# A graph network layer: the one-hots of gathered rows move from VectorE to GpSimd, a turn later, with the flags of used slots copied beside the row numbers

## The chip, the cores and the metric

The program runs on one core of a Trainium2 chip. The metric is the device time of one execution in microseconds (us). A core has the engines TensorE (PE in the profile; PEld is its weight load), VectorE (DVE), ScalarE (ACT), GpSimd (POOL) and SyncE (SP), which each work through a queue of their own in order and meet through semaphores.

## The reference

25,000 edges with sorted source nodes (`src` here is the row that sums go to) and 50,000 nodes of width 256.

```python
h = concat([x[row], x[col]])                      # 25000 x 512
msgs = silu(h @ W1.T + b1) @ W2.T + b2
agg = segment_sum(msgs, row) / (cnt + 1e-8)       # per node
gi, gh = agg @ w_ih.T + b_ih, x @ w_hh.T + b_hh   # 3 x 256 each
r, z = sigmoid(i_r + h_r), sigmoid(i_z + h_z)
n = tanh(i_n + r * h_n)
x_new = (1 - z) * n + z * x
y = gamma * (x_new - mean) / sqrt(var + 1e-5) + beta
out = layernorm(x + y)
```

## The kernel before

The work has two stages. The **edge stage** (to about 955 us) turns each edge into a message that is already multiplied by W2 and w_ih, and stores it in DRAM as one row of `messages`. It also makes a table: for each block of 128 nodes up to 126 slots, with the row of an edge in `slot_row` and a flag in `slot_used` that says whether the slot holds an edge. The **node stage** handles the nodes in 196 pairs of blocks, one pair in a turn of the loop `node_turns`. For a pair and each of its two halves (`h`), GpSimd gathers 126 message rows by an indirect DMA into `mg`. A one-hot matrix `oh` then says for each gathered row which of the 128 nodes it belongs to: row `i` compares `iota1` with the local node number that the message carries in column `LOC`, and multiplies by the flag. TensorE multiplies `oh` by `mg` (`segment_sum`), which adds each edge to its node, and then adds the products of x with w_hh into the same banks of PSUM (`products0`, `products1`).

Each engine runs its own list of parts in a turn. A part comes with a lag: at turn t it handles pair t + lag, so that a part with lag 4 works four pairs ahead. Nothing but the semaphores holds the engines together. The parts that matter here, in the order of a turn:

- POOL: `add_beta` (lag -2, xb = x + beta; it waits for the second gate of pair t-1, `n_rz1`), `gather_rows` (lag 4; at every second turn `copy_rows` first copies four columns of row numbers into `rows_now`), `inv_std1` (-2, every second turn) and `inv_std2` (-5), which raise a variance to the power -0.5 (rs in the trace).
- DVE: `gated_h` and `n_input` (-1; rhn and npre), `var_eps2` (-5), `residual` (-4, uu), `one_hot` (3), `minus_mean` (nm), `subtract_n`, `z_diff`, `x_new` (diff, zd, xn), `scale_gamma` (tg), `stats1` (st), `shift` (-5, nmr; a product of two 128x2 tiles that waits for rs of `inv_std2`), `aggregate1` (ag), and `var_eps1` at every second turn (ve<-ag).
- ACT: `last_norm` (-6, yy<-uu,nmr; it waits for nmr), `tanh` (-1; it waits for npre), `gates0` (0), `mean_scale` (1), `squares` (-4), `gates1` (0, rz).
- PE: `products0` (0), `segment_sum` (1; it waits for the one-hots and for npre of pair t-1, since the banks are two sets), `products1` (0).

In what follows a turn with even t (in which GpSimd copies row numbers) is called even, and the other odd.

Of the kernel before, what the change touches and what calls it, by code (L numbers as in the profile page):

```python
# [7 lines left out]
P = 128  # L8
# [55 lines left out]
def gnn_layer(nc, x, xt, src, dst, w1t, b1, w2, b2, wiht, whht, bih, bhh, gamma, beta, consts, out):  # L64
# [4 lines left out]
    with ctx:  # L69
        def sb(name, shape, dt=f32, until=ctx):  # L70
            return until.enter_context(nc.sbuf_tensor(name, shape, dt))

        def sem(name):
            return ctx.enter_context(nc.semaphore(name))
# [25 lines left out]
        gammab, betab = sb("gammab", [P, D]), sb("betab", [P, 2 * D])  # L100
        rows_now = sb("rows_now", [P, 2 * QU], i32)
        halves = sb("halves", [P, 4])
        top, levf, levi = sb("top", [P, 1]), sb("levf", [1, 1]), sb("levi", [1, 1], i32)
        levels = sb("levels", [1, 1], i32)

# [58 lines left out]
        rb_mm, rb_cp, rb_step, rb_ready = sem("rb_mm"), sem("rb_cp"), sem("rb_step"), sem("rb_ready")  # L164
        cn_ready, cn_mm, cn_cp, cn_put = sem("cn_ready"), sem("cn_mm"), sem("cn_cp"), sem("cn_put")

        idx_now = sem("idx_now")
        got_src, got_dst, e_stored = sems("got_src", XE), sems("got_dst", XE), sems("e_stored", EU)
        e_xt, e_hi, e_lo = sem("e_xt"), sem("e_hi"), sem("e_lo")
        e_hid, e_sil, e_sh, e_sl = sems("e_hid", KC), sems("e_sil", KC), sems("e_sh", KC), sems("e_sl", KC)  # L170
# [18 lines left out]
        def need(eng, s, value):  # L189
            if not isinstance(value, int) or value > 0:  # L190
                eng.wait_ge(s, value)  # L191
# [37 lines left out]
        def duo(q, u):  # L229
            return q // 2 + 1 if isinstance(q, int) else (q - u) // 2 + u // 2 + 1  # L230

        def node_turns(eng, parts, first, last):
            def step(q, u):
                for part, lag in parts:
                    if not isinstance(q, int) or 0 <= q + lag < PAIRS:
                        part(q + lag, (u + lag) % QU)

            head = QU * (-(min(lag for _, lag in parts) // QU) + 1)
            tail = PAIRS - QU * -(-max(lag for _, lag in parts) // QU)
            for q in range(first, head):  # L240
                step(q, q % QU)
            with eng.Fori(head // QU, tail // QU) as g:
                for u in range(QU):
                    step(g * QU + u, u)
            for q in range(tail, PAIRS + last):
                step(q, q % QU)
# [104 lines left out]
        @block.gpsimd  # L351
        def _(pool):
            last_row = pool.to_reg(EDGES_PAD - 1)
            pool.wait_ge(ld_e, 32)

            def gather_edges(t0, turn_no, side):
                if not isinstance(turn_no, int) or turn_no >= 2:
                    for u in range(XE):
                        pool.wait_ge(got_dst[u], 16 * (turn_no - 1))
                nc.gpsimd.tensor_copy(src_now[:, side, :], srci[:, bass.ds(t0, XE)]).then_inc(idx_now, 1)  # L360
                nc.gpsimd.tensor_copy(dst_now[:, side, :], dsti[:, bass.ds(t0, XE)]).then_inc(idx_now, 1)
                pool.wait_ge(idx_now, 2 * turn_no + 2)
                for u in range(XE):
                    need_apart(pool, pool_passed, e_xt, t0 + (u - XE + 1))
                    gather(xsrc[:, u, :], src_now[:, side, u:u + 1], x, got_src[u])
                    gather(xdst[:, u, :], dst_now[:, side, u:u + 1], x, got_dst[u])

            E_TURNS = TILES // XE
            gather_edges(0, 0, 0)
            nc.gpsimd.memset(halves[:, :], -0.5).then_inc(node_const, 1)  # L370
            with pool.Fori(0, E_TURNS // 2) as g:
                for side in range(2):
                    gather_edges((g * 2 + (side + 1)) * XE, g * 2 + (side + 1), (side + 1) % 2)

            for u in range(EU):
                pool.wait_ge(e_stored[u], 16 * (TILES // EU))
            pool.wait_ge(tab_ready, 1)
            pool.wait_ge(mg_zero, 2 * QU)

            def node_stage(summed):  # L380
                def copy_rows(q, u):
                    need(pool, S["n_oh"], q - QU + 2)
                    nc.gpsimd.tensor_copy(rows_now[:, 2 * u:2 * u + 4], slot_row[:, bass.ds(2 * q, 4)])\  # L383
                        .then_inc(idx_now, 1)
                    pool.wait_ge(idx_now, 2 * E_TURNS + duo(q, u))

                def gather_rows(q, u):
                    if u % 2 == 0 and not summed:
                        copy_rows(q, u)
                    for h in range(2):  # L390
                        to = mg[:, u, h, :].bitcast(f32)
                        need_apart(pool, pool_passed, S[f"n_sg{h}"], q - QU + 1)
                        if summed:
                            nc.gpsimd.dma_start(to, sums[h][bass.ds(q * P, P), :])\
                                .then_inc(got_m[2 * u + h], 16)
                        else:
                            gather(to, rows_now[:, 2 * u + h:2 * u + h + 1], messages, got_m[2 * u + h], last_row)

                def add_beta(q, u):

                    pool.wait_ge(S["n_rz1"], min(q + 2, PAIRS) if isinstance(q, int) else q + 2)
                    need(pool, S["n_u"], q - QU + 1)
                    pool.wait_ge(got_x[u], 16 * (nth(q, u) + 1))
                    nc.gpsimd.tensor_tensor(out=xb[:, u, :], in0=xs[:, u, :], in1=betab[:, :], op=ALU.add)\  # L404
                        .then_inc(S["n_xb"], 1)

                def inv_std1(q, u):
                    if u % 2 == 1:
                        pool.wait_ge(S["n_v1"], duo(q, u))
                        need(pool, S["n_u"], q - QU + 1)  # L410
                        nc.gpsimd.tensor_tensor(
                            out=rs1[:, u - 1:u + 1, :].rearrange("p q h -> p (q h)"),
                            in0=ve1[:, u - 1:u + 1, :].rearrange("p q h -> p (q h)"),
                            in1=halves[:, :], op=ALU.pow).then_inc(S["n_r1"], 1)

                def inv_std2(q, u):
                    pool.wait_ge(S["n_v2"], q + 1)
                    need(pool, S["n_y"], q - QU + 1)
                    nc.gpsimd.tensor_tensor(out=rs2[:, u, :], in0=ve2[:, u, :], in1=halves[:, 0:2], op=ALU.pow)\
                        .then_inc(S["n_r2"], 1)  # L420

                node_turns(pool, ((add_beta, -2), (gather_rows, 4), (inv_std1, -2), (inv_std2, -5)), first=-4, last=5)

            pool.wait_ge(ld_w, 16 * W_LOADS)
            pool.wait_ge(lv_ready, 1)
            n_levels = pool.value_load(levels[0:1, 0:1], min_val=1, max_val=MAX_LEVELS)
            with pool.If(n_levels > 1):
                with pool.Fori(0, n_levels) as lv:
                    with pool.Fori(0, BLOCKS) as b:
                        n = lv * BLOCKS + b  # L430
                        pool.wait_ge(v_rows, lv + 1)
                        pool.wait_ge(v_sum, n + 1)
                        nc.gpsimd.tensor_copy(rows_now[:, 0:1], slot_row[:, bass.ds(b, 1)]).then_inc(v_idx, 1)
                        need_apart(pool, pool_passed, v_idx, n + 1)
                        gather(mg[:, 0, 0, :].bitcast(f32), rows_now[:, 0:1], messages, v_got, last_row)
                pool.wait_ge(v_done, 1)
                pool.wait_ge(tab_ready, 2)
                node_stage(True)
            with pool.Else():
                node_stage(False)  # L440
# [106 lines left out]
        def _(dve):  # L547
# [243 lines left out]
                nc.vector.memset(slot_used[:, :], 1.0).then_inc(tab_ready, 1)  # L791
                dve.wait_ge(tab_ready, 2)

            def one_hot(q, u):
                for h in range(2):
                    need(dve, S[f"n_sg{h}"], q - QU + 1)
                    dve.wait_ge(got_m[2 * u + h], 16 * (nth(q, u) + 1))
                    last = nc.vector.tensor_scalar(oh[0:SLOTS, u, h, :], iota1[0:SLOTS, :],  # L798
                                                   mg[0:SLOTS, u, h, LOC:LOC + 1].bitcast(f32),
                                                   slot_used[0:SLOTS, bass.ds(q * 2 + h, 1)], ALU.is_equal, ALU.mult)  # L800
                last.then_inc(S["n_oh"], 1)

            def gated_h(q, u):
                dve.wait_ge(S["n_rz0"], q + 1)
                dve.wait_ge(S["n_rz1"], q + 1)
# [74 lines left out]
            def var_eps1(q, u):  # L880
                if u % 2 == 1:
# [1 line left out]
                    nc.vector.tensor_scalar(ve1[:, u - 1:u + 1, :], ag1[:, u - 1:u + 1, :, 1], EPS_LN, None, ALU.add)\  # L883
                        .then_inc(S["n_v1"], 1)

            node_turns(dve, ((gated_h, -1), (n_input, -1), (var_eps2, -5), (residual, -4), (one_hot, 3), (minus_mean, -4),
                             (subtract_n, -1), (z_diff, -1), (x_new, -1), (scale_gamma, -3), (stats1, -1), (shift, -5),
                             (aggregate1, -1), (var_eps1, -1)), first=-3, last=5)

        @block.tensor  # L890
        def _(pe):
# [193 lines left out]
```

## Time and profile before

| | |
|---|---|
| time, median of 3 | 2478.14 us (2478.11 to 2478.32) |
| the profiled execution | 2478.47 us, of which the span of its instructions is 2476.8 us |
| PE busy | 2301.0 us (93%) |
| DVE busy | 2122.0 us (86%) |
| ACT busy | 1496.2 us (60%) |
| POOL busy | 1332.4 us (54%) |
| granted TensorE clock, mean | 0.987 |

The chain in the page (the work that ended last, followed backwards) gives DVE 42% and PE 37% of the span. Busy time counts an instruction from its start to its end, also where it stands still in between. The interval from one xb on POOL to the next is one turn of the node stage.

### The profile page before, as it was taken

The numbers are of one execution on the slowest core, as the hardware profiler recorded it, in microseconds if no ns is written. First come the engines' busy times: TensorE is split into PE (matmuls) and PEld (weight loads), VectorE is DVE, ScalarE is ACT, GpSimd is POOL, SyncE is SP. The second block draws the span as 40 slices with busy tenths as digits, with TensorE's granted clock in tenths as the row PEclk, the third lists the DMA queues.
The fourth block names the chain that finished last, engine by engine and source line by source line (L and its number), as shares of the span: only waits on it lengthen the run. The fifth ranks groups of instructions, "written<-read, shape, count | busy, mean of one in ns | idle before, by whom it ended". The sixth has DMA issues, their size and how long they took to land.

```text
span 2476.8 us, 46628 instructions
## 1 busy us (share of the span) xinstructions
PE 2301.0 (93%) x10234; PEld 1622.0 (65%) x10234; DVE 2122.0 (86%) x6136; ACT 1496.2 (60%) x2955; POOL 1332.4 (54%) x1475
## 2 busy tenths in 40 slices
PE   4999999999999995999999999999999999999995
PEld 2888888888888883655555555555555555555553
DVE  4777777777777764899999999999999999999998
ACT  2444444444444442577767777777677777777776
POOL 3444444444444421566666666666666666666663
PEclk9999999999999997999999999999999999999998
DMA  3566666666666655666666666666666666666662
GB/s 105 213 232 227 229 230 228 230 227 231 225 233 225 234 209 193 200 216 216 213 210 213 214 217 205 216 207 210 203 212 213 210 205 212 215 209 212 209 204 94
DMA packets 192600, 520.31 MB, mean 210 GB/s; under 512 B 51362, under 2 KB 53946, under 8 KB 192572
## 3 DMA queue, kind: packets, MB, share of 16 engines
q1 hardware_dynamic: 117308, 313.53, 36.2%
q0 software_dynamic: 75264, 206.47, 25.5%
q8 instruction: 9, 0.15, 0.0%
q14 instruction: 19, 0.16, 0.0%
HBM read 468.02 MB, written 206.73 MB: 272 GB/s over the span
## 4 chain that ended last, share of the span: by engine, by line
DVE 42%; PE 37%; issue 15%; DVEq 3%; DMA 1%; ACT 1%; SPq 0%; POOL 0%; POOLq 0%; ACTq 0%
PE banks L893 34%; DVE zd L824 6%; DVE xn L830 5%; DVE st L871 5%; DVE diff L819 5%; DVE rhn L807 5%; DVE tg L835 4%; DVE uu L846 4%; PE banks L905 4%; DVE oh L798 3%; DVE ag L877 2%; DVE ve L860 1%; DVEq L798 1%; DVEq L191 1%; DVE nm L855 1%
## 5 line engine op out<-in xcount | busy, mean ns | idle before, releaser
L893 PE MATMUL banks<-whh,xts 128*128 128x512 f32 (+1 forms) x3136 | 1089.9, 485 | 0.0
L893 PEld LDWEIGHTS banks<-whh,xts 128*128 128x128 f32 x3136 | 552.4, 190 | 312.5 <-issue 281.7
L346 POOL DMA_INDIRECT mg<-messages,rows_now x392 | 408.1, 1041 | 170.4 <-POOL rows_now L383 87.1
L404 POOL TENSOR_TENSOR xb<-xs,betab 128x512 f32<-128x512 f32 x196 | 249.0, 1270 | 372.5 <-ACT rz L501 372.5
L346 POOL DMA_INDIRECT xsrc<-in_x,src_now x196 | 187.3, 956 | 438.5 <-PE banks L905 433.0
L893 PE MATMUL banks<-mg,oh 128*128 128x512 f32 (+1 forms) x1568 | 322.1, 348 | 108.7 <-issue 57.2
L893 PEld LDWEIGHTS banks<-mg,oh 128*128 128x128 f32 x1568 | 253.2, 189 | 214.9 <-issue 158.7
L525 ACT ACTIVATE yy<-uu,nmr,rs 128x256 f32<-128x256 f32 x392 | 214.0, 593 | 293.0 <-DVE nmr L866 293.0
L513 ACT ACTIVATE banks<-banks,rcount 128x768 f32<-128x768 f32 x392 | 326.7, 871 | 38.0 <-PE banks L893 24.9
L471 ACT ACTIVATE msg<-banks 128x512 fp32r<-128x512 f32 (+1 forms) x392 | 192.8, 492 | 246.7 <-PE banks L893 218.3
L625 DVE TENSOR_TENSOR msg<-banks,msg 128x512 fp32r<-128x512 f32 (+1 forms) x392 | 199.9, 552 | 160.1 <-issue 137.7
L893 PE MATMUL banks<-wsh,silh 128*128 128x512 f32 (+1 forms) x784 | 265.1, 338 | 2.9 <-DVE msg L625 2.9
L893 PE MATMUL banks<-bias_hn,ones 128*128 128x256 f32 x392 | 267.5, 682 | 0.0
L893 PE MATMUL banks<-wsh,sill 128*128 128x512 f32 (+1 forms) x784 | 263.8, 336 | 0.0
L893 PE MATMUL banks<-wsl,silh 128*128 128x512 f32 (+1 forms) x784 | 263.4, 336 | 0.0
L501 ACT ACTIVATE rz<-banks 128x512 f32<-128x512 f32 x392 | 229.3, 585 | 3.0 <-PE banks L893 3.0
L452 ACT ACTIVATE eh<-banks 128x512 fp32r<-128x512 f32 x196 | 117.5, 599 | 172.2 <-PE banks L905 172.2
L346 POOL DMA_INDIRECT xdst<-in_x,dst_now x196 | 186.0, 949 | 65.2 <-issue 65.2
L519 ACT ACTIVATE nt<-npre 128x512 f32<-128x512 f32 x196 | 123.9, 632 | 119.3 <-issue 76.3
L535 ACT ACTIVATE yy<-uu,nm 128x256 f32<-128x256 f32 x392 | 194.6, 503 | 1.9 <-DVE nm L855 1.9
L866 DVE TENSOR_TENSOR nmr<-nm,rs 128x2 f32<-128x2 f32 x196 | 179.6, 916 | 0.8 <-ACT yy L525 0.8
L846 DVE SCALAR_TENSOR_TENSOR uu<-tg,rs,xb 128x256 f32<-128x256 f32 x392 | 173.5, 480 | 0.0
(129 smaller groups left out, 4248.8 us busy)
## 6 DMA issues: line engine op xcount, KB each, us to landing
messages<-msg SPq DMA_DIRECT2D x196, 772.0 KB
xts<-in_xt SPq DMA_DIRECT2D x196, 256.0 KB
xs<-in_x SPq DMA_DIRECT2D x196, 256.0 KB
out_y<-yy SPq DMA_DIRECT2D x196, 256.0 KB, 5.1
mg<-messages,rows_now POOLq DMA_INDIRECT x392
xsrc<-in_x,src_now POOLq DMA_INDIRECT x196
xdst<-in_x,dst_now POOLq DMA_INDIRECT x196
oh<-counts SPq DMA_DIRECT2D x196, 2.0 KB
```

What stands on the lines that cost most here:

```text
L346: nc.gpsimd.indirect_dma_start(out=dst_tile, out_offset=None, in_=rows, in_offset=bass.IndirectOffsetOnAxis(ap=table, axis=0), bounds_chec ...
L404: nc.gpsimd.tensor_tensor(out=xb[:, u, :], in0=xs[:, u, :], in1=betab[:, :], op=ALU.add)\
L471: nc.scalar.activation(msg[:, u % EU, n0:n1], p_g[:, part, 0:n1 - n0], ACT.Copy).then_inc(e_gh[part], 1)
L501: nc.scalar.activation(rz[:, u % 2, h, :], pn[u % 2][:, h, 0, :], ACT.Sigmoid).then_inc(S[f"n_rz{h}"], 1)
L513: nc.scalar.activation(sums_now, sums_now, ACT.Copy, scale=rcount[:, bass.ds(q * 2 + h, 1)])\
L525: last = nc.scalar.activation(yy[:, u, h * D:(h + 1) * D], uu[:, u, h * D:(h + 1) * D], ACT.Identity, bias=nmr[:, u, h:h + 1], scale=rs2[: ...
L535: last = nc.scalar.activation(yy[:, u, h * D:(h + 1) * D], uu[:, u, h * D:(h + 1) * D], ACT.Square, bias=nm2[:, u, h:h + 1], accum_out=sq2 ...
L625: nc.vector.tensor_tensor(msg[:, u % EU, HALF + n0:HALF + n1], p_g[:, part, 0:n1 - n0], msg[:, u % EU, n0:n1].bitcast(f32), ALU.subtract). ...
L824: nc.vector.tensor_tensor(zd[:, u % 2, :].rearrange("p (h d) -> p h d", h=2), rz[:, u % 2, :, D:2 * D], diff[:, u % 2, :].rearrange("p (h ...
L846: last = nc.vector.scalar_tensor_tensor(out=uu[:, u, h * D:(h + 1) * D], in0=tg[:, u % 2, h * D:(h + 1) * D], scalar=rs1[:, u, h:h + 1], i ...
L866: nc.vector.tensor_tensor(nmr[:, u, :], nm2[:, u, :], rs2[:, u, :], ALU.mult).then_inc(S["n_nmr"], 1)
L893: return nc.tensor.matmul(out_, lhsT, rhs, start=start, stop=stop, skip_group_check=skip)
```

## The change

VectorE no longer makes the one-hots. GpSimd makes them, with lag 2 in place of 3, right behind `add_beta` and ahead of the gathers. The flags come as a tile, `used_now`, that GpSimd copies from `slot_used` beside each copy of row numbers. The steps of a turn on VectorE now begin at turn 0.

```diff
@@ node_stage, on GpSimd
                 def copy_rows(q, u):
                     need(pool, S["n_oh"], q - QU + 2)
+                    nc.gpsimd.tensor_copy(used_now[:, 2 * u:2 * u + 4], slot_used[:, bass.ds(2 * q, 4)])\
+                        .then_inc(used_ready, 1)
                     nc.gpsimd.tensor_copy(rows_now[:, 2 * u:2 * u + 4], slot_row[:, bass.ds(2 * q, 4)])\
                         .then_inc(idx_now, 1)
...
+                def one_hot(q, u):
+                    for h in range(2):
+                        need(pool, S[f"n_sg{h}"], q - QU + 1)
+                        pool.wait_ge(used_ready, duo(q, u))
+                        need_apart(pool, pool_passed, got_m[2 * u + h], 16 * (nth(q, u) + 1))
+                        last = nc.gpsimd.tensor_scalar(oh[0:SLOTS, u, h, :], iota1[0:SLOTS, :],
+                                                       mg[0:SLOTS, u, h, LOC:LOC + 1].bitcast(f32),
+                                                       used_now[0:SLOTS, 2 * u + h:2 * u + h + 1], ALU.is_equal, ALU.mult)
+                    last.then_inc(S["n_oh"], 1)
...
-                node_turns(pool, ((add_beta, -2), (gather_rows, 4), (inv_std1, -2), (inv_std2, -5)), first=-4, last=5)
+                node_turns(pool, ((add_beta, -2), (one_hot, 2), (gather_rows, 4), (inv_std1, -2), (inv_std2, -5)), first=-4, last=5)
@@ on VectorE
-            def one_hot(q, u):
-                for h in range(2):
-                    need(dve, S[f"n_sg{h}"], q - QU + 1)
-                    dve.wait_ge(got_m[2 * u + h], 16 * (nth(q, u) + 1))
-                    last = nc.vector.tensor_scalar(oh[0:SLOTS, u, h, :], iota1[0:SLOTS, :],
...
-            node_turns(dve, ((gated_h, -1), (n_input, -1), (var_eps2, -5), (residual, -4), (one_hot, 3), (minus_mean, -4),
+            node_turns(dve, ((gated_h, -1), (n_input, -1), (var_eps2, -5), (residual, -4), (minus_mean, -4),
                              (subtract_n, -1), (z_diff, -1), (x_new, -1), (scale_gamma, -3), (stats1, -1), (shift, -5),
-                             (aggregate1, -1), (var_eps1, -1)), first=-3, last=5)
+                             (aggregate1, -1), (var_eps1, -1)), first=0, last=5)
```

The even turn on POOL before, inside the loop (xb is x + beta, mg the gathered rows, rs the inverse deviation; a REGISTER_ALU or ISA row computes or loads a register):

```order
L404 TENSOR_TENSOR xb<-xs,betab 128x512
L383 ISA
L383 COPY rows_now<-slot_row 128x4
L385 REGISTER_ALU
L191 REGISTER_ALU
L346 DMA mg<-messages,rows_now 128x1544 x2
L417 REGISTER_ALU
L191 REGISTER_ALU
L419 TENSOR_TENSOR rs<-ve,halves 128x2
```

The same turn of the change, from the two one-hots that now follow xb to the end of the turn:

```order
L415 TENSOR_SCALAR oh<-iota,mg,used_now 126x128 x2
L384 ISA
L384 COPY used_now<-slot_used 128x4
L386 REGISTER_ALU
L386 COPY rows_now<-slot_row 128x4
L388 REGISTER_ALU
L192 REGISTER_ALU
L347 DMA mg<-messages,rows_now 128x1544 x2
L430 REGISTER_ALU
L192 REGISTER_ALU
L432 TENSOR_TENSOR rs<-ve,halves 128x2
```

Two one-hots now stand between xb and the gathers, and at even turns one copy more; rs follows behind all of them, as the last instruction of the turn.

On DVE, a turn of the loop before, from uu to nmr (one ISA row and one one-hot for each half):

```order
L846 SCALAR_TENSOR_TENSOR uu,usum<-tg,rs,xb 128x256 x2
L798 ISA
L798 TENSOR_SCALAR oh<-iota,mg,slot_used 126x128
L798 ISA
L798 TENSOR_SCALAR oh<-iota,mg,slot_used 126x128
L855 TENSOR_SCALAR nm<-usum 128x2
L819 TENSOR_TENSOR diff<-xs,nt 128x512
L824 TENSOR_TENSOR zd<-rz,diff 128x512
L830 TENSOR_TENSOR xn<-zd,nt 128x512
L835 SCALAR_TENSOR_TENSOR tg<-xn,ag,gammab 128x256 x2
L871 BN_STATS st<-xn 128x6 x2
L866 TENSOR_TENSOR nmr<-nm,rs 128x2
```

The same stretch of the change:

```order
L851 SCALAR_TENSOR_TENSOR uu,usum<-tg,rs,xb 128x256 x2
L860 TENSOR_SCALAR nm<-usum 128x2
L824 TENSOR_TENSOR diff<-xs,nt 128x512
L829 TENSOR_TENSOR zd<-rz,diff 128x512
L835 TENSOR_TENSOR xn<-zd,nt 128x512
L840 SCALAR_TENSOR_TENSOR tg<-xn,ag,gammab 128x256 x2
L876 BN_STATS st<-xn 128x6 x2
L871 TENSOR_TENSOR nmr<-nm,rs 128x2
```

nm now follows uu at once, and everything to nmr keeps its order.

## Rows read from the trace of the kernel before

**Rows 1.** The page's busy times: engine, us, share of the span, instructions.
```profile
PE 2301.0 (93%) x10234; PEld 1622.0 (65%) x10234; DVE 2122.0 (86%) x6136; ACT 1496.2 (60%) x2955; POOL 1332.4 (54%) x1475
```

**Rows 2.** Who waited for whom, 1010 to 2410 us: us in total, times, longest.
```profile
POOL xb L404 <- ACT rz L501: 350.4, 186, 3.5
ACT yy L525 <- DVE nmr L866: 277.8, 184, 1.8
...
PE banks L893 <- DVE npre L813: 27.5, 57, 0.6
```

**Rows 3.** Timeline of two turns: start us, duration us, engine, line, operation [idle before].
```profile
1598.97 1.27 POOL L404 TENSOR_TENSOR xb<-xs,betab 128x512 f32<-128x512 f32 x1 [1.96 <-ACT rz L501]
...
1603.72 0.75 POOL L419 TENSOR_TENSOR rs<-ve,halves 128x2 f32<-128x2 f32 x1
...
1606.15 1.26 POOL L404 TENSOR_TENSOR xb<-xs,betab 128x512 f32<-128x512 f32 x1 [1.68 <-ACT rz L501]
...
1606.59 0.84 DVE L866 TENSOR_TENSOR nmr<-nm,rs 128x2 f32<-128x2 f32 x1
...
1607.74 0.69 DVE L807 TENSOR_TENSOR rhn<-rz,banks 128x512 f32<-128x512 f32 x1
...
1608.47 0.69 DVE L813 TENSOR_TENSOR npre<-rhn,banks 128x512 f32<-128x512 f32 x1
...
1609.95 0.08 DVE L846 DVE_READ_ACCUMULATOR uu<-tg,rs,xb 128x1 f32 x1
...
1610.54 0.69 DVE L819 TENSOR_TENSOR diff<-xs,nt 128x512 f32<-128x512 f32 x1
...
1611.01 0.78 POOL L419 TENSOR_TENSOR rs<-ve,halves 128x2 f32<-128x2 f32 x1
...
1613.02 0.58 ACT L501 ACTIVATE rz<-banks 128x512 f32<-128x512 f32 x1
...
1613.91 1.26 POOL L404 TENSOR_TENSOR xb<-xs,betab 128x512 f32<-128x512 f32 x1 [2.13 <-ACT rz L501]
1614.06 1.14 DVE L866 TENSOR_TENSOR nmr<-nm,rs 128x2 f32<-128x2 f32 x1
```

**Rows 4.** Timeline of three early turns, before the first nmr.
```profile
1016.33 1.27 POOL L404 TENSOR_TENSOR xb<-xs,betab 128x512 f32<-128x512 f32 x1 [1.90 <-ACT rz L501]
...
1016.74 0.69 DVE L807 TENSOR_TENSOR rhn<-rz,banks 128x512 f32<-128x512 f32 x1
...
1023.26 1.26 POOL L404 TENSOR_TENSOR xb<-xs,betab 128x512 f32<-128x512 f32 x1 [2.06 <-ACT rz L501]
...
1023.55 1.00 DVE L883 TENSOR_SCALAR ve<-ag 128x4 f32<-128x4 f32 x1
...
1030.21 1.44 POOL L404 TENSOR_TENSOR xb<-xs,betab 128x512 f32<-128x512 f32 x1 [1.25 <-ACT rz L501]
```

**Rows 5.** Timeline of a late turn in which DVE has no one-hots left.
```profile
2441.78 0.08 DVE L846 DVE_READ_ACCUMULATOR uu<-tg,rs,xb 128x1 f32 x1
...
2441.98 0.69 DVE L819 TENSOR_TENSOR diff<-xs,nt 128x512 f32<-128x512 f32 x1
```

**Rows 6.** Timeline of the last turns: DVE and POOL against each other.
```profile
2453.86 0.14 DVE L866 TENSOR_TENSOR nmr<-nm,rs 128x2 f32<-128x2 f32 x1
...
2457.06 0.69 DVE L819 TENSOR_TENSOR diff<-xs,nt 128x512 f32<-128x512 f32 x1
2457.08 1.80 POOL L404 TENSOR_TENSOR xb<-xs,betab 128x512 f32<-128x512 f32 x1
...
2457.79 1.64 DVE L824 TENSOR_TENSOR zd<-rz,diff 128x512 f32<-128x512 f32 x1
```

**Rows 7.** Groups by line, 1010 to 2410 us: count, busy us, mean ns, idle before.
```profile
L404 POOL TENSOR_TENSOR xb<-xs,betab 128x512 f32<-128x512 f32 x188 | 238.1, 1266 | 350.4 <-ACT rz L501 350.4
...
L419 POOL TENSOR_TENSOR rs<-ve,halves 128x2 f32<-128x2 f32 x185 | 145.6, 787 | 2.1
...
L798 DVE TENSOR_SCALAR oh<-iota,mg,slot_used 126x128 fp32r<-126x128 f32 x374 | 113.1, 344 | 0.2
...
L383 POOL COPY rows_now<-slot_row 128x4 int32 (+1 forms) x93 | 17.2, 185 | 0.0
```

More of the change, by code:

```diff
@@ L102, in gnn_layer @@
         halves = sb("halves", [P, 4])
+        used_now = sb("used_now", [P, 2 * QU])
         top, levf, levi = sb("top", [P, 1]), sb("levf", [1, 1]), sb("levi", [1, 1], i32)
@@ L165, in gnn_layer @@
         cn_ready, cn_mm, cn_cp, cn_put = sem("cn_ready"), sem("cn_mm"), sem("cn_cp"), sem("cn_put")
-        idx_now = sem("idx_now")
+        idx_now, used_ready = sem("idx_now"), sem("used_ready")
         got_src, got_dst, e_stored = sems("got_src", XE), sems("got_dst", XE), sems("e_stored", EU)
@@ L437, in _ @@
                 pool.wait_ge(tab_ready, 2)
+                nc.gpsimd.memset(used_now[:, :], 1.0).then_inc(used_ready, PAIRS // 2)
                 node_stage(True)
@@ L792, in _ @@
                 dve.wait_ge(tab_ready, 2)
-            def one_hot(q, u):
-                for h in range(2):
-                    need(dve, S[f"n_sg{h}"], q - QU + 1)
-                    dve.wait_ge(got_m[2 * u + h], 16 * (nth(q, u) + 1))
-                    last = nc.vector.tensor_scalar(oh[0:SLOTS, u, h, :], iota1[0:SLOTS, :],
-                                                   mg[0:SLOTS, u, h, LOC:LOC + 1].bitcast(f32),
-                                                   slot_used[0:SLOTS, bass.ds(q * 2 + h, 1)], ALU.is_equal, ALU.mult)
-                last.then_inc(S["n_oh"], 1)
             def gated_h(q, u):
```

## The prediction

> **What bounds the kernel now.** I read the busy times first, to see which engines can be the limit; then the waits, to see who waits; then the timeline of two turns, to see why.
>
> The busy times name PE (93%) and DVE (86%) [rows 1]. Taken at its word that makes DVE a limit of the node stage, and two instructions fewer on it a gain. The waits say that it isn't so simple: POOL's xb waits for ACT's gate rz (350.4 us), ACT's last step waits for DVE's nmr (277.8 us), and PE now and then for npre (27.5 us) [rows 2]. So the engines go round in a loop. The timeline shows it [rows 3]. nmr is a product of two 128x2 tiles, and the same instruction takes 0.14 us when POOL is quiet [rows 6]. In the two turns it takes 0.84 and 1.14 us, and ends at 1607.43 and 1615.20, where POOL's xb ends (1607.41 and 1615.17). It stands still behind xb. In the last turns the same is seen of zd: it starts at 2457.79 behind an xb that runs to 2458.88, and takes 1.64 us where its neighbours take 0.69; and that xb itself took 1.80 us where 1.27 is usual, since diff was running when it came [rows 6, 7]. Whoever comes first keeps the other out, and a waiting one gets in when the other ends.
>
> The loop of a turn is then: xb ends at 1607.41 and lets nmr go; rhn starts at 1607.74, npre ends at 1609.16; ACT works through its list to rz, which ends at 1613.60; xb starts at 1613.91 and ends at 1615.17 [rows 3]. That is 7.76 us from xb's end to the next; the even turn before it took 7.17 (1600.24 to 1607.41). The mean over the stage is (2457.08 - 1030.21) / 191 turns = 7.471 us [rows 4, 6]. The one-hots are not in this loop. They lie on DVE between npre and nmr, and nmr arrives behind xb's start anyhow: 0.44 us late in one turn, 0.15 in the other [rows 3].
>
> What a turn costs without the lock-out of nmr is in the trace too: before the first nmr, xb starts at 1016.33, 1023.26 and 1030.21, so 6.93 and 6.95 us apart [rows 4]. In the second of these ve stood still behind xb for 1.00 us, and the turn didn't get longer for it. PE, with little to wait for in those turns, is then the likely limit. I take **6.94 us** as the turn that is to be had.
>
> **The change, part by part.**
>
> *Removed from DVE.* From the end piece of uu to diff it is 0.59 us with one-hots (1609.95 to 1610.54 [rows 3]) and 0.20 without (2441.78 to 2441.98 [rows 5]). So DVE comes to nmr 0.39 us earlier, not by the 0.69 that two times 344 ns [rows 7] would make, as they overlap. Against the offsets above that is -0.24 us in the turn in which it was 0.15 late (nmr gets in before xb) and still 0.05 late in the other. When nmr gets in, about 1 us is saved on DVE at once, rhn starts as soon as the gate is there, and in the next turn nmr comes about a microsecond before xb. So one win leads to the next, as long as nmr's other input is there.
>
> *Added to POOL.* That other input is rs, POOL's last instruction of a turn. Now it ends 5.50 us behind the start of xb in the even turn (1598.97 to 1604.47) and 5.64 in the odd one (1606.15 to 1611.79) [rows 3]. Ahead of it come two one-hots and, at even turns, a copy. The copy costs 0.19 us [rows 7]. For a 126x128 TENSOR_SCALAR on POOL there is no row. Below it lies the copy of four elements, 0.185 us, above it the addition of 512 elements from two inputs, 1.27; on DVE it takes 0.34 [rows 7]. A line through the two POOL rows gives 0.185 + 124/508 x 1.08 = 0.45 us for 128 elements, and I take that. The other side is open: a power over two elements takes 0.79 us [rows 7], so the operation itself can matter. POOL's turn is then 5.50 + 0.19 + 0.90 = 6.59 (even) and 5.64 + 0.90 = 6.54 (odd), with 0.1 to 0.2 for gaps between instructions about 6.7. That leaves 0.2 us to a turn of 6.94.
>
> The Trainium skill, page GPSIMD Engine Reference, section Performance versus the Vector engine, puts a two-input pass at about 2.6 cycles an element and small one-input bodies at about 1. By that page an estimate for the one-hot would be 0.3 us and POOL's turn about 6.4.
>
> *The lock, met by the new instructions.* In a fast turn the one-hots run from about 1.3 to 2.3 us behind xb's start, and uu, which reads two tiles, comes on DVE at about 1.6 (rhn with the gate, npre's end 1.42 later as from 1607.74 to 1609.16). Each can hold up the other. On DVE that is at most both one-hots, 0.9 us; about 0.6, since DVE comes when the first is under way. DVE's work in a turn without nmr's standstill is 6.38 us: 6.63 from the end of nmr to the start of the next (1607.43 to 1614.06), less 0.39, and 0.14 for nmr itself. With 0.6 it would be 6.98, just the turn. The later DVE comes, the less it meets of them. rhn itself ran its 0.69 us under an xb unhindered [rows 4], so the start of the turn is safe. I put 0.04 us a turn on all this.
>
> *Waits.* The one-hot of pair t+2 waits on POOL for rows that were sent for two turns earlier, some 14 us; DVE waited for rows sent for one or two turns earlier and lost 0.2 us in the whole stage [rows 7]. Hidden. PE needs it a full turn later. The gathers behind it start 0.9 us later with four turns to spare. In the first turns GpSimd holds back its third and fourth gather until rows have landed; PE waits for the first one-hots anyhow. I allow 1 us.
>
> *Sum.* 6.94 + 0.04 = 6.98 us a turn against 7.471: 0.49 x 191 = 94 us less, 1 more at the start: 2478.5 (the profiled execution) - 93 = 2385.5. The profiled execution is 0.3 above the median; I say **2385 us**.
>
> **The rivals.**
>
> *Part of it.* POOL's turn ends just when the gate does. Then xb starts right behind rs, and nmr, released by that same rs, comes second. Such a turn costs 7.2 to 7.5, the next is free again: a mean of 7.1 to 7.4. That happens if a one-hot with its gap takes 0.55 to 0.8 us. 191 x 0.37 down to 191 x 0.07: 2405 to 2465. For it: the spare 0.2 us is less than my doubt about the one-hot.
>
> *No change.* nmr never gets in before xb, since POOL's turn still fits and ACT's chain sets the pace: 7.47 and 2478. For it: 0.05 us late in one of two turns. Against it: the 0.15 turn.
>
> *Slower, by POOL's length.* The turn of POOL is 5.57 + 0.1 + two one-hots with gaps. From 0.9 us for one with its gap on it passes 7.47 and decides alone. At 1.0 us: 7.67, +0.2 x 191 = 38: 2516. The power rows speak for it, the addition against it.
>
> *Slower, by the lock.* nmr still lands behind xb, and now the first one-hot starts as xb ends. At odd turns ve comes behind nmr and ag, about 0.3 us behind xb's end and just ahead of rhn (0.33 us behind it); xb could hold it up [rows 4], so a one-hot can. One of 0.45 with a gap of 0.1 ends at 0.55, so that ve and rhn are some 0.26 us late, inside the loop. Every second turn: 0.13 x 191 = +25: 2503. The Trainium skill, page SBUF — State Buffer, section Who interferes with whom, states that one instruction keeps the shared port pair to its end and the other fully blocks. Rows 6 agree. [...]
>
> **How the numbers follow.** Forecast 0.40 (2368 to 2402, for 6.9 to 7.07 a turn); part of it 0.25; no change 0.09; slower by length 0.14; slower by the lock 0.12. About 0.2% (5 us) is what a measurement can tell. Faster 0.65, same 0.09, slower 0.26. The range runs from a turn of 6.9 to the price of the lock: 2368 to 2508; above it I leave most of the slower-by-length case and some of the lock, below it a faster PE turn than any seen.
>
> **What would show it.** In the profile after: nmr near 0.15 us in the mean, where it is 0.84 and 1.14 now; xb to xb 6.9 to 7.1 us; one-hots on POOL near 0.45 us; rs ending before the gate; PE's waits for npre gone. nmr at 0.8 with rs ending just ahead of xb means part of it. xb with no idle time before it means that POOL is the limit. ve or uu much longer than the same instructions before means the lock. The forecast is wrong above all if the one-hot takes more than 0.5 us.

## The result: slower by 2.7%, and GpSimd no longer idle ahead of xb

The changed kernel takes 2546.65 us (median of 4 runs, 2541.69 to 2548.74), the kernel before 2478.12: a ratio of 1.0274 (95% interval 1.0261 to 1.0286). The profiled execution took 2548.74 us with a span of 2547.1. The mean granted clock of TensorE was 0.983, before 0.987: 0.4% less, and TensorE's own busy time is 2304.0 us in place of 2301.0, so the clock doesn't account for 2.7%. The prediction said 2385 us, faster.

The page's busy times after, and a line of its chain of work that ended last:

```profile
PE 2304.0 (90%) x10234; PEld 1627.4 (64%) x10234; DVE 2110.8 (83%) x5744; ACT 1495.8 (59%) x2955; POOL 1761.1 (69%) x1965
...
PE 46%; POOL 25%; issue 21%; DVE 5%; POOLq 2%; ACT 0%; DMA 0%; SPq 0%; DVEq 0%; ACTq 0%
```

GpSimd (POOL) is busy 429 us more than in [rows 1], VectorE (DVE) only 11 less although it has 392 instructions fewer. In the chain, DVE has gone from 42% to 5% and POOL has 25%. At 69% POOL still looks like an engine with room. The waits from 1010 to 2480 us (total us, times, longest) say otherwise:

```profile
ACT yy L539 <- DVE nmr L871: 320.6, 181, 4.0
PEld banks L898 <- POOL oh L415: 144.4, 111, 3.6
...
PE banks L898 <- DVE npre L818: 112.7, 94, 3.2
POOL mg L347 <- PE banks L898: 84.0, 92, 1.0
...
POOL xb L407 <- ACT rz L515: 4.3, 4, 1.1
```

xb waited for the gate rz for 350.4 us [rows 2]; that is now 4.3 us in all. POOL hardly waits for another engine any more, and TensorE (PE) waits for it. The 84.0 us that the view puts down to PE are the 0.9 us behind each copy of row numbers; they were there before too, 82.9 us in 91 times, put down to POOL's own copy. Its turn in the timeline (start us, duration us; the value in brackets is the idle time before):

```profile
1605.38 1.26 POOL L407 TENSOR_TENSOR xb<-xs,betab 128x512 f32<-128x512 f32 x1
1606.63 1.59 POOL L415 TENSOR_SCALAR oh<-iota,mg,used_now 126x128 fp32r<-126x128 f32 x2
1608.40 1.13 POOL L347 DMA_INDIRECT mg<-messages,rows_now  x1 [0.18 <-issue]
1609.84 1.33 POOL L347 DMA_INDIRECT mg<-messages,rows_now  x1 [0.31 <-issue]
1611.18 1.47 POOL L424 TENSOR_TENSOR rs<-ve,halves 128x4 f32<-128x4 f32 x1
1612.65 0.69 POOL L432 TENSOR_TENSOR rs<-ve,halves 128x2 f32<-128x2 f32 x1
1613.36 1.27 POOL L407 TENSOR_TENSOR xb<-xs,betab 128x512 f32<-128x512 f32 x1
```

This is an odd turn, without copies. The two one-hots take 1.59 us. Every instruction starts as the one ahead ends, but for the gaps that each gather has, 0.18 and 0.31 us. DVE's and ACT's side of the same stretch:

```profile
1605.43 1.38 DVE L871 TENSOR_TENSOR nmr<-nm,rs 128x2 f32<-128x2 f32 x1 [0.22 <-POOL rs L432]
...
1607.20 0.69 DVE L812 TENSOR_TENSOR rhn<-rz,banks 128x512 f32<-128x512 f32 x1
...
1609.61 0.69 DVE L824 TENSOR_TENSOR diff<-xs,nt 128x512 f32<-128x512 f32 x1
1610.33 0.69 DVE L829 TENSOR_TENSOR zd<-rz,diff 128x512 f32<-128x512 f32 x1
1611.06 0.69 DVE L835 TENSOR_TENSOR xn<-zd,nt 128x512 f32<-128x512 f32 x1
1611.67 0.87 DVE L840 SCALAR_TENSOR_TENSOR tg<-xn,ag,gammab 128x256 f32<-128x256 f32 x2
...
1612.47 0.59 ACT L515 ACTIVATE rz<-banks 128x512 f32<-128x512 f32 x1
```

The gate ends at 1613.06 (1612.47 + 0.59), 0.30 us ahead of the second xb: POOL wasn't ready for it. nmr was there in time and waited 0.22 us for rs. But xb, next on POOL's own list, starts as rs ends, gets in first, and nmr stands still until it is over. So it goes in nearly every turn: of the 185 nmr below, 28 took less than 0.3 us. The groups from 1010 to 2480 us (count, busy us, mean ns, idle before), against [rows 7]:

```profile
L347 POOL DMA_INDIRECT mg<-messages,rows_now x374 | 451.4, 1207 | 161.5 <-PE banks L898 84.0 <-issue 73.9 <-DVE uu L851 2.7
L415 POOL TENSOR_SCALAR oh<-iota,mg,used_now 126x128 fp32r<-126x128 f32 x375 | 301.7, 806 | 0.1
...
L424 POOL TENSOR_TENSOR rs<-ve,halves 128x4 f32<-128x4 f32 x94 | 136.3, 1450 | 2.2
L432 POOL TENSOR_TENSOR rs<-ve,halves 128x2 f32<-128x2 f32 x185 | 132.1, 714 | 2.1
L386 POOL COPY rows_now<-slot_row 128x4 int32 x89 | 34.0, 382 | 0.0
...
L871 DVE TENSOR_TENSOR nmr<-nm,rs 128x2 f32<-128x2 f32 x185 | 209.9, 1135 | 56.4 <-POOL rs L432 56.4
```

The one-hot costs 0.81 us where I took 0.45. And three kinds of instruction that the change doesn't touch take longer. In the kernel before the gathers' mean was 1.043 us and that of the 128x4 power 1.095:

```profile
L346 POOL DMA_INDIRECT mg<-messages,rows_now x378 | 394.1, 1043 | 163.7 <-POOL rows_now L383 83.8 <-issue 56.1 <-DVE uu L846 23.8
...
L411 POOL TENSOR_TENSOR rs<-ve,halves 128x4 f32<-128x4 f32 x98 | 107.3, 1095 | 6.6 <-DVE ve L883 4.3
```

The mean turn, from the xb at 1029.94 to that at 2527.32, 191 turns, is 7.840 us, where it was 7.471. 0.369 x 191 = 70.5 us, which is the whole difference of the spans (70.3).

### The profile page after: what moved, and what is told of

Its sections match the earlier page's. It is cut to its first block, busy times and chain, and to the rows that moved or that the text cites. A ratio compares the mean times of both kernels' runs of the same rounds, so it can differ in the third digit from the quotient of the medians.

```text
span 2547.1 us, 46948 instructions
## 1 busy us (share of the span) xinstructions
PE 2304.0 (90%) x10234; PEld 1627.4 (64%) x10234; DVE 2110.8 (83%) x5744; ACT 1495.8 (59%) x2955; POOL 1761.1 (69%) x1965
## 4 chain that ended last, share of the span: by engine, by line
PE 46%; POOL 25%; issue 21%; DVE 5%; POOLq 2%; ACT 0%; DMA 0%; SPq 0%; DVEq 0%; ACTq 0%
PE banks L898 42%; POOL mg L347 10%; POOL oh L415 7%; POOL rs L424 4%; PE banks L910 3%; POOL rs L432 3%; DVE rhn L812 1%; POOL rows_now L386 1%; POOL xb L407 1%; DVE npre L818 1%; DVE uu L851 1%; POOLq L192 1%; POOLq L196 0%; DVE ag L882 0%; POOL used_now L384 0%
## 5 line engine op out<-in xcount | busy, mean ns | idle before, releaser
L347 POOL DMA_INDIRECT mg<-messages,rows_now x392 | 470.7, 1201 | 169.4 <-PE banks L898 85.8
L415 POOL TENSOR_SCALAR oh<-iota,mg,used_now 126x128 fp32r<-126x128 f32 x392 | 315.7, 807 | 3.9 <-issue 3.4
L871 DVE TENSOR_TENSOR nmr<-nm,rs 128x2 f32<-128x2 f32 x196 | 216.7, 1105 | 57.6 <-POOL rs L432 56.8
L347 POOL DMA_INDIRECT xdst<-in_x,dst_now x196 | 185.9, 949 | 65.2 <-issue 65.2
```

The lines of the kernel that those rows point to most:

```text
L347: nc.gpsimd.indirect_dma_start(out=dst_tile, out_offset=None, in_=rows, in_offset=bass.IndirectOffsetOnAxis(ap=table, axis=0), bounds_chec ...
L415: last = nc.gpsimd.tensor_scalar(oh[0:SLOTS, u, h, :], iota1[0:SLOTS, :], mg[0:SLOTS, u, h, LOC:LOC + 1].bitcast(f32), used_now[0:SLOTS, 2 ...
L871: nc.vector.tensor_tensor(nmr[:, u, :], nm2[:, u, :], rs2[:, u, :], ALU.mult).then_inc(S["n_nmr"], 1)
```

## The experiments

Each was timed beside the kernel before (medians 2476.9 to 2477.6 us). "Turn" is the mean distance of xb from xb over the last 191 turns of the profiled execution. The theory behind the first runs: POOL's length is the bound, through the one-hot's price. The rivals: the lock of the SBUF port between DVE and POOL, the copies of flags, the shorter lag.

### One-hots gone from VectorE, and not on GpSimd either

```
-  (residual, -4), (one_hot, 3), (minus_mean, -4),      # DVE, kernel before
+  (residual, -4), (minus_mean, -4),
+  pe.wait_ge(got_m[2 * u], ...); pe.wait_ge(got_m[2 * u + 1], ...)
```

oh is filled once with an identity, so no one-hots are computed.

> The kernel before with no one-hots made in the node stage at all, neither on VectorE nor on GpSimd: each slot of oh is filled once with rows of the identity, so the sums are not those of the reference. TensorE and the copies of row numbers wait for the gathered rows instead. It isolates what VectorE gains. The prediction's first step (0.39 us off VectorE lets nmr in ahead of xb, one win leads to the next) expects about 2385 us, xb to xb near 6.95 us and nmr near 0.15 us. The rival (nmr keeps landing behind xb, the loop through ScalarE sets the pace) expects 2440 to 2478 us with nmr near 0.8 to 1.2 us.

2405.77 us, ratio 0.9716 (0.9695 to 0.9736); turn 7.08. This is the half of the change that takes work off DVE: it gives 71 us, where the forecast had 93. nmr is let in early in many turns, not in all, and at some odd turns the `ve` behind it now stands still in its place (0.54 us in the mean, before 0.19):

```profile
L868 DVE TENSOR_TENSOR nmr<-nm,rs 128x2 f32<-128x2 f32 x196 | 76.2, 389 | 3.3 <-POOL rs L420 2.5 <-ACT yy L526 0.8
...
L885 DVE TENSOR_SCALAR ve<-ag 128x4 f32<-128x4 f32 x98 | 53.1, 542 | 3.4
```

So the gain was there to be had, and what GpSimd was given to do took about 140 us against it (2546.65 - 2405.77 = 140.9).

### The price of the one-hot: one operation, and a quarter of the columns

```
-  used_now[0:SLOTS, 2 * u + h:2 * u + h + 1], ALU.is_equal, ALU.mult)   # the change
+  None, ALU.is_equal)                                                   # no flag
```
```
-  nc.gpsimd.tensor_scalar(oh[0:SLOTS, u, h, :], iota1[0:SLOTS, :],      # the change
+  nc.gpsimd.tensor_scalar(oh[0:SLOTS, u, h, 0:32], iota1[0:SLOTS, 0:32],
```

The first leaves the flags out of the one-hots, the second leaves three quarters of each one-hot at zero.

> The change with one operation in GpSimd's one-hot (is_equal alone) in place of two, so without the product with the flag; empty slots then add stale rows. It tells what the second operation and its operand cost. If each operation costs as much, the one-hot falls from 0.80 to about 0.5 us and the total to 2440 to 2480 us; if the operand's fetch is small, it stays above 0.7 us and the total above 2510 us.

> The change with GpSimd's one-hots cut from 128 to 32 columns (the other 96 stay zero, so most sums are missing). It measures how the 0.80 us of a one-hot on GpSimd divide into a fixed part and a part for each element. If all of it goes by elements as in the addition (about 2 ns an element), it falls to about 0.6 us; if mostly by elements, to 0.3 us; if fixed, it stays 0.8. Theory L then expects GpSimd's turn shorter by twice the difference and a total of 2546 minus 196 times that, until the limit of the loop, 2440 to 2480 us.

```profile
L415 POOL TENSOR_SCALAR oh<-iota,mg 126x128 fp32r<-126x128 f32 x380 | 228.5, 608 | 0.0
```
```profile
L415 POOL TENSOR_SCALAR oh<-iota,mg,used_now 126x32 fp32r<-126x32 f32 x380 | 179.7, 476 | 0.0
```

Without the flag 2476.59 us, ratio 0.9998 (0.9988 to 1.0007), turn 7.50; with 32 columns 2467.29, ratio 0.996 (0.9945 to 0.9974), turn 7.42. From 806 to 476 ns over 96 columns is 3.4 ns a column. If the price goes by columns in a straight line, which two widths can't show, 0.37 us are left that don't go by columns. The second operation with its operand is 0.20 us. A turn falls by 0.34 us for 0.40 us less of one-hots, and by 0.42 for 0.66: nearly one for one as long as POOL is full, then less, since xb then has to wait for the gate in a part of the turns (75.2 and 89.1 us in the two runs).

### Half of the one-hots each

```
-  for h in range(2):            # GpSimd's one_hot, the change
+  for h in range(1, 2):         # VectorE makes h = 0 again, with lag 3
```

> The change with only the second half's one-hot on GpSimd; the first half's stays on VectorE with lag 3 as before. GpSimd's turn loses one instruction of 0.80 us. Theory L (GpSimd's turn of 7.82 us decides) expects GpSimd's turn near 7.0 us and so the next limit: the loop with nmr behind xb, 7.2 to 7.5 us, 2430 to 2480 us, or 2385 us if nmr gets in. If the lock between VectorE and GpSimd rather than the length made the change slow, half of the loss stays: about 2510 us.

2452.87 us, ratio 0.9905 (0.9888 to 0.9921), turn 7.33. One one-hot a turn fits, since xb still waits for the gate here (102.7 us in all); two don't. nmr stays behind xb (mean 0.85 us).

### The one-hots at the end of GpSimd's turn

```
-  ((add_beta, -2), (one_hot, 2), (gather_rows, 4), (inv_std1, -2), (inv_std2, -5))
+  ((add_beta, -2), (gather_rows, 4), (inv_std1, -2), (inv_std2, -5), (one_hot, 2))
```

> The change with one_hot moved from behind add_beta to the end of GpSimd's turn, so that rs is ready 1.6 us earlier while GpSimd does the same work. Theory L expects no gain: 2530 to 2550 us, xb with no idle time before it. Theory K (nmr's standstill because rs comes late) expects nmr ahead of xb, near 0.15 us, and most of the loss gone: 2400 to 2480 us.

```profile
L407 POOL TENSOR_TENSOR xb<-xs,betab 128x512 f32<-128x512 f32 x192 | 243.2, 1267 | 5.1 <-ACT rz L515 5.1
...
L865 DVE TENSOR_SCALAR ve<-sq 128x2 f32<-128x2 f32 x190 | 161.7, 851 | 0.0
...
L871 DVE TENSOR_TENSOR nmr<-nm,rs 128x2 f32<-128x2 f32 x190 | 33.3, 175 | 58.1 <-POOL rs L432 58.1
```

2512.81 us, ratio 1.0145 (1.0128 to 1.0162), turn 7.66. With one-hots between rs and xb, nmr gets in (0.175 us, where the change has 1.135), and yet the kernel is slower than before. xb has no idle time before it, so POOL's length sets the turn by itself. nmr's standstill isn't what makes the change slow. VectorE isn't rid of standing still, though: the `ve` between npre and uu now meets xb and takes 0.85 us in the mean, where the kernel before has 0.16. The time lies outside the ranges of both theories, 17 us below that of Theory L. Of the 0.18 us a turn that the move gives, 0.11 are the 128x4 power's (1.235 us in place of 1.450, every second turn) and 0.02 the one-hots' (0.796 each); the rest I haven't placed.

### xb cut to 16 of its 512 columns

```
-  nc.gpsimd.tensor_tensor(out=xb[:, u, :], in0=xs[:, u, :], in1=betab[:, :], op=ALU.add)
+  nc.gpsimd.tensor_tensor(out=xb[:, u, 0:16], in0=xs[:, u, 0:16], in1=betab[:, 0:16], op=ALU.add)
```

It leaves out nearly all of x + beta.

> The change with GpSimd's xb = x + beta cut from 512 to 16 columns (the other columns of xb stay zero, so the residual is left out of most of the output). It takes about 1.1 us from GpSimd's turn and the long lock-out of VectorE with it. Theory L expects GpSimd's turn at about 6.7 us and the total at 2380 to 2400 us, TensorE being next. If the two engines' lock on the one-hots themselves costs a large part, the total stays above 2430 us.

2355.44 us, ratio 0.9509 (0.9493 to 0.9525), turn 6.84. The one-hots still cost 0.80 us each, the gathers 1.18, the 128x4 power 1.41; but with 1.05 us taken from POOL's turn the kernel is 5% faster than the one before. PE's waits (the engine's list, 1010 to 2480 us) are down to one line:

```profile
PE banks L899 <- DVE npre L819: 2.7, 3, 1.3
```

PE is busy for 799.16 of the 800 us from 1500 to 2300, so PE is the limit here, as the prediction supposed: the floor of 6.94 us that it took from three early turns was sound, 0.1 too high. This run takes xb's length from POOL's turn and from the lock at once (nmr 0.18 us), so it doesn't part the two; the run before it does.

### The copies of flags alone, and the shorter lag alone

```
+  nc.gpsimd.tensor_copy(used_now[:, 2 * u:2 * u + 4], slot_used[...])   # kernel before, copies only
```
```
-  (one_hot, 3)        # DVE, kernel before
+  (one_hot, 2)
```

> The kernel before plus only the copies of the flags beside the row numbers on GpSimd (nobody reads them; the one-hots stay on VectorE). GpSimd idles about 1.9 us ahead of xb in each turn there, so 0.18 us at every second turn should be hidden: 2478 us, within 0.2%. If every us of GpSimd's turn counts, 98 x 0.18 = +18 us.

> The kernel before with only the lag of VectorE's one_hot changed from 3 to 2, the part of the change that makes the one-hots a turn later. TensorE needs them a turn later still, so no change: 2470 to 2482 us. If TensorE came to wait for them, as it does on GpSimd in the change, it would be slower than 2490 us.

2474.15 us, ratio 0.9991 (0.9981 to 1.0001), and 2473.28, ratio 0.9983 (0.9974 to 0.9993). Neither part costs anything; the lag may give 0.2%.

### Who stands behind whom: four kernels on nmr's standstill

The first, on the kernel before, has VectorE's `shift` ahead of `scale_gamma`. The second makes xb wait for nmr and ve of DVE's previous turn, and the third is the second with the one-hots at lag 2. The fourth is the half-and-half kernel with both edits.

```
-  (x_new, -1), (scale_gamma, -3), (stats1, -1), (shift, -5),       # first
+  (x_new, -1), (shift, -5), (scale_gamma, -3), (stats1, -1),
```
```
   need(pool, S["n_u"], q - QU + 1)                                 # second, add_beta
+  need(pool, S["n_nmr"], q - 3)
+  if u % 2 == 1:
+      pool.wait_ge(S["n_v1"], duo(q, u))
```

> The kernel before, with shift (nmr) moved on VectorE from behind stats1 to ahead of scale_gamma, about 1.4 us earlier; nothing else. Theory K (what a turn costs beyond 6.95 us is nmr's standstill behind xb) expects nmr near 0.15 us, 6.9 to 7.05 us a turn and 2375 to 2400 us. Theory L (only the length of the queues of GpSimd and VectorE counts) expects no change, 2478 us, since no work is taken from any engine.

> The kernel before, with the one-hots on VectorE, and one more wait for xb on GpSimd: for nmr (and ve at odd turns) of VectorE's turn before. So xb runs under ag, rhn and npre, none of which it held up in the trace of before. No work is moved. If nmr's standstill is what the turn costs beyond 6.95 us, 2375 to 2420 us; if the standstill only moves to another instruction, as it did with shift moved earlier, 2470 us or more.

> The kernel before with xb waiting for nmr (and ve) of VectorE's turn before, as in the run of that edit alone, and VectorE's one_hot with lag 2 in place of 3. In that run nmr was free at 0.15 us and turns of 6.9 to 7.1 us stood beside long ones, in which the one-hots waited for rows that the later gathers had not landed. If that wait is what ate the gain, 2380 to 2410 us; if TensorE or ScalarE's chain holds the turn anyhow, 2450 us or more.

> One half's one-hot on GpSimd and one on VectorE as in the run of that edit (VectorE's now with lag 2), and xb waiting for nmr and ve of VectorE's turn before. GpSimd's turn is about 6.7 us, and rs to nmr to xb adds 0.2: about 7.0 us a turn and 2395 to 2415 us. If the order of rs, nmr and xb costs GpSimd more than the lock-out costs VectorE, it is above the 2453 us of the half alone.

The first: 2488.74 us, ratio 1.0054 (1.0037 to 1.007). nmr takes 0.17 us, but what follows it takes its place:

```profile
1606.17 0.16 DVE L866 TENSOR_TENSOR nmr<-nm,rs 128x2 f32<-128x2 f32 x1 [0.62 <-POOL rs L419]
1606.24 1.90 DVE L835 SCALAR_TENSOR_TENSOR tg<-xn,ag,gammab 128x256 f32<-128x256 f32 x2
1606.47 1.39 POOL L404 TENSOR_TENSOR xb<-xs,betab 128x512 f32<-128x512 f32 x1 [0.34 <-ACT rz L501]
```

The theories expected 2375 to 2400 us (K) and 2478 (L), and neither came. The two tg take 1.90 us in place of 0.87 (tg's mean over the stage is 0.58 where it was 0.48): the second half stands behind xb. The second kernel: 2483.05, ratio 1.0028 (1.0016 to 1.004), turn 7.50. Nothing stands behind xb any more, but DVE's one-hots now wait for their rows; the third ends that by the shorter lag. Waits of the second (us, times, longest), and of the third:

```profile
DVE oh L801 <- DMA mg<-messages,rows_now: 45.3, 56, 1.9
```
```profile
POOL xb L407 <- DVE ve L886: 133.3, 95, 4.8
...
POOL xb L407 <- DVE nmr L869: 53.2, 96, 3.6
```

The third takes **2401.22 us, ratio 0.9694 (0.9677 to 0.971)**, turn 7.09, and is the fastest kernel here that computes all of the reference. It gives xb a wait of 186 us in all and gains 76, although its gathers (1.198 us) and its 128x4 power (1.457) are as long as those of the change. POOL has room there, since the one-hots are on DVE. The fourth is the counter-test: 2515.82 us, ratio 1.016 (1.0143 to 1.0177). Turn 7.69. With one one-hot on POOL and the same order forced, nmr waits 171.6 us for rs, and xb waits for nmr behind it: POOL's list is then one leg of a loop, rs to nmr to xb. My expectation had missed that. The one-hot itself takes 0.94 us here; it lies under uu.

### What stretches the gathers, the power and the copy

What stayed open was the second part of POOL's length. In the change the second gather at 1609.84 lies under diff, zd on DVE, the power at 1611.18 under xn and tg; all these read two SBUF tiles. Two kernels replace such operations by a `bn_stats` over one tile, of nearly the same length (0.70 us for 128x512; for 128x256 0.41 in place of 0.48). Both leave out what these operations compute.

```
-  nc.vector.tensor_tensor(diff[:, u % 2, :], xs[:, u, :], nt[:, u % 2, :], ALU.subtract)
+  nc.vector.bn_stats(dum[:, 0, :], xs[:, u, :])
```
The same for zd and xn; in the second kernel for the two halves of tg and of uu too.

> The change with the three VectorE operations of the middle of the turn that read two SBUF tiles (diff, zd, xn, each 128x512) replaced by bn_stats over one tile of the same shape; what they compute is left out. The tiles, waits and order stay. Theory A (GpSimd's gathers, its 128x4 power and its row copy take longer because they lie under VectorE operations with two SBUF inputs): the gather's mean falls from 1.21 us to about 1.04, the 128x4 power from 1.45 to about 1.10, the copy from 0.38 to about 0.19, the turn from 7.84 to about 7.3, the median to 2420 to 2460. Theory B (they take longer because of something else, such as the one-hots ahead of them on the same engine or the DMA traffic): the durations stay within 5% of those of the change, the turn stays at 7.7 to 7.9, the median at 2520 to 2550.

> As the run before, and the four halves of scale_gamma and shift (tg and uu, two SBUF tiles read by each) are bn_stats over one tile too, so that no wide VectorE operation with two SBUF inputs is left in the node stage; what they compute is left out. Theory A: also nmr no longer stands behind xb (mean 0.15 instead of 1.14 us), the one-hot's 0.81 us stays if it is the operation's own price and falls if part of it was contention, xb's 1.28 us likewise; turn 7.1 to 7.3, median 2370 to 2430. Theory B: durations on GpSimd as in the change; nmr alone may shorten; GpSimd is still full, so the turn stays at 7.6 to 7.9 and the median at 2500 to 2550.

The groups of the first:

```profile
L348 POOL DMA_INDIRECT mg<-messages,rows_now x380 | 415.0, 1092 | 164.7 <-PE banks L902 86.6 <-issue 76.9 <-DVE uu L851 1.2
...
L425 POOL TENSOR_TENSOR rs<-ve,halves 128x4 f32<-128x4 f32 x94 | 99.3, 1056 | 2.2
L385 POOL COPY used_now<-slot_used 128x4 f32 x90 | 37.9, 421 | 0.0
L387 POOL COPY rows_now<-slot_row 128x4 int32 x90 | 28.5, 316 | 0.0
```

And of the second:

```profile
L348 POOL DMA_INDIRECT mg<-messages,rows_now x380 | 406.8, 1070 | 164.7 <-PE banks L899 85.9 <-issue 77.9 <-POOL rows_now L387 0.8
L416 POOL TENSOR_SCALAR oh<-iota,mg,used_now 126x128 fp32r<-126x128 f32 x382 | 303.1, 796 | 0.1
L408 POOL TENSOR_TENSOR xb<-xs,betab 128x512 f32<-128x512 f32 x195 | 247.1, 1267 | 65.3 <-ACT rz L516 65.2
...
L425 POOL TENSOR_TENSOR rs<-ve,halves 128x4 f32<-128x4 f32 x98 | 103.0, 1051 | 5.2 <-DVE ve L883 2.9
L385 POOL COPY used_now<-slot_used 128x4 f32 x90 | 16.2, 180 | 0.0
L387 POOL COPY rows_now<-slot_row 128x4 int32 x90 | 16.0, 177 | 0.0
```

Theory A holds for the durations. Once diff, zd and xn read one tile, gathers (1.09 us) and power (1.06) are nearly as short as before the change; the copies, which lie under uu, stay long until uu reads one tile too. The one-hot (0.80) and xb (1.27) don't change, so these are the operations' own prices. A `bn_stats` also writes 6 columns where the operations in whose place it stands write 256 or 512, so the two kernels by themselves don't part reading from writing. The change does: its one-hots lie under rhn and npre, which write 512 columns to SBUF and read only one tile from it (the other is in PSUM), and cost 0.81 us there and 0.80 in the second kernel. On the time Theory A's numbers failed. The first kernel takes 2537.03 us, ratio 1.0245 (1.0228 to 1.0262), turn 7.77, the second 2479.5, ratio 1.0007 (0.9997 to 1.0017), turn 7.47, and I had expected 2420 to 2460 and 2370 to 2430. In the first, POOL's busy time a turn falls from 7.02 to 6.71 us (busy sums of its groups by the turns), but the turn only by 0.07: in 92 turns of 189 xb now waits for the gate, 0.54 us each. So the loop in which nmr stands behind xb is itself nearly as long as POOL's list, and taking time from POOL uncovers it. In the second it is 6.32 busy and 0.33 waiting (65.2 us over 195 xb). nmr is still let in only in every second turn:

```profile
L866 DVE TENSOR_TENSOR nmr<-nm,rs 128x2 f32<-128x2 f32 x196 | 130.8, 667 | 111.0 <-POOL rs L433 110.1 <-ACT yy L540 0.8
```

## Why the prediction was wrong

**What bounds the kernel.** Right. The loop xb, nmr, rhn, npre, rz was the bound before; making room on DVE alone gives 2.8%, and forcing nmr ahead of xb, with the one-hots left on DVE at lag 2, gives 3.1%. The order without the lag gives nothing (+0.3%), the lag without the order 0.2%.

**The turn that is to be had, 6.94 us.** Right within 0.1 as a floor: 6.84 with xb cut short and PE always busy. No kernel here that computes all of the reference gets below 7.09.

**Removed from DVE.** Right in direction and too hopeful in size. That "one win leads to the next" isn't so: without any one-hots nmr's mean is 0.39 us and the turn 7.08, not 6.94. That is 0.39 us less than before, what the one-hots took on DVE and no more; where nmr gets in, the next standstill is that of ve.

**Added to POOL, the step that failed.** "A line through the two POOL rows gives 0.185 + 124/508 x 1.08 = 0.45 us for 128 elements, and I take that." It measured 0.806. The copy and the addition are other operations; the row that should have counted was the one I put aside, the power over two elements at 0.79 us, which says that on POOL the operation and its operands have a price of their own. By the two widths that is 0.37 us fixed and 3.4 ns a column. By itself this makes POOL's turn 5.57 + 0.09 + 1.61 = 7.27 us in place of 6.6. The sum had 0.2 us of room, as the text of the part-of-it rival said; it needed 0.7. The estimate that the prediction worked out from the Trainium skill (GPSIMD Engine Reference, section Performance versus the Vector engine: 0.3 us for the one-hot) was further off: the trace has 0.81.

**The lock, met by the new instructions, and what was missing from the sum.** The prediction priced the lock between the one-hots and uu only, at 0.04 us, and took POOL's other instructions at their durations of before. They moved later by the one-hots' 1.6 us and came to lie under uu, diff, zd, xn and tg, all with two inputs in SBUF. Gathers 2 x 0.164, power 0.178, copy 0.098, less 0.073 for the 128x2 power, which now lies under st: 0.53 us a turn. 7.27 + 0.53 = 7.80 against the measured 7.84. This adds up POOL's list, which is what the turn consists of as long as xb doesn't wait. It isn't what the turn would shrink by: of the 0.31 us that the first one-input kernel takes off the list, the turn gives back 0.07. That these are the operations which stretch them is shown by the last two kernels. The Trainium skill, page SBUF — State Buffer, section Who interferes with whom, states that a `tensor_tensor` of VectorE with both inputs in SBUF contends with GpSimd's reads; the rows of the one-input kernels agree (power 1.45 to 1.05 us, copy 0.38 to 0.18).

**The rivals.** "Slower, by POOL's length" is what happened, at 0.14. Its threshold, 0.9 us for one one-hot with its gap, held POOL's other instructions at their old durations, and at 0.81 it wasn't reached: the kernel in which they have those durations stands at 2479.5 us, no slower than before. The other 67 us (2546.65 - 2479.5) come with the two-input operations; that kernel also has shorter standstills of nmr and about 0.3 us less work a turn on VectorE (four times 0.07), so not all of them need be POOL's. "Slower, by the lock" had the sign and another place: rhn wasn't held up by the one-hots (0.67 us, as before) and ve only a little (0.24 us in the mean, before 0.19), and with xb no longer waiting for the gate neither sets the turn. Of the signs that the prediction named, "xb with no idle time before it means that POOL is the limit" is the one that came; nmr at 1.135 is "part of it" at its worst, since nmr's last input and xb's start are now the same event in nearly every turn.

**Waits.** Right in part: for its rows the one-hot on POOL waits 0.1 us in the whole stage, and flags and lag cost nothing. PE's wait for the one-hots, which the prediction had put off with "PE needs it a full turn later", is 37.3 us of matmuls and 144.4 of weight loads; it is there since POOL as a whole is late: with xb cut to 16 columns, at the same lag, it falls to nothing and 9.2 us.

**Still open.** How much of the 7.47 us of the last kernel is loop and how much POOL: it has both a full POOL in one turn and a wait for the gate in the next. For the same reason the loss in the change isn't split between the stretched instructions and nmr's standstill.

## What to carry to other kernels

An engine that waits for its first instruction of a turn has about as much room as that wait before the turn gets longer, here 1.9 us of 7.5, not what its busy share of 54% says; set the added work against the wait, with a price for the operation on that very engine, and measure the operation if no row has it. When work is put ahead of other instructions on GpSimd, price those again by what VectorE does at the place where they land: under two-input VectorE operations a gather, a power and a copy took 1.2, 1.3 and 2 times as long in the mean. And where a short instruction of the critical loop stands behind a long one that needn't come first, the better cure may be the order: holding xb back for two tiny VectorE results gave 3.1% once the one-hots came a turn later (nothing without that), where moving 0.7 us of work to the other engine lost 2.7%.

## What the runs showed of the hardware

- A `tensor_scalar` of GpSimd over 126x128 with two scalars read from SBUF takes 0.81 us, with one scalar and one operation 0.61, over 32 columns 0.48; VectorE takes 0.34 for the first [rows 7].
- Operations of GpSimd as small as a copy of four elements take 0.38 us in place of 0.18 under a two-input VectorE operation, a gather's instruction 1.33 in place of 1.00 to 1.13. To have begun first doesn't always help: in the change the gather at 1603.63 ran its 1.00 us beside a tg that began at 1603.67, but in the kernel with xb behind nmr and lag 2 the gather at 1196.30, which began 0.01 us ahead of diff with zd behind it, took 1.57.
- rhn and npre, which read one tile from PSUM, ran their 0.69 us under xb and under one-hots in every kernel.
